# Turning softmax probabilities on one Trainium2 core: a matmul with a scaled diagonal, or a float32 transpose after a GpSimd multiply

## The chip, the cores and the metric

One core of a Trainium2 chip runs the whole kernel. It has a matrix engine (TensorE, PE in the profile; PEld is its weight load), a vector engine (VectorE, DVE), an activation engine (ScalarE, ACT), GpSimd (POOL), and SyncE (SP), which here only issues DMA transfers. Each engine works through its own queue in order and waits on semaphores. The metric is the device time of one execution in microseconds.

## The reference

Four sequences of 512 rows of 512 values (x), and a context of 512 rows of 256 values for each. With LN a layer norm without weights and q(.) a quantization to fp8 with one scale for each 32 values:

```
query = ctx @ Wq.T + bq ;  key = ctx @ Wk.T + bk            (512 x 128 each)
attention = softmax(query @ key.T, axis=-1)                 (512 x 512)
x = x + LN(x) @ attention.T
gate = q(LN(x)) @ q(gate_w).T ;  up = q(LN(x)) @ q(up_w).T  (2048 columns each)
x = x + q(silu(gate) * up) @ q(down_w).T
```

All of it in float32 accuracy. Attention is row n by column m; the product with LN(x) sums over m, so the probabilities have to be turned: m must be on the partitions.

## The kernel before

The kernel is written for each engine as one list of calls whose order was fixed by hand or by a planner; semaphores tie the lists together. b is the sequence (0 to 3), nt a tile of 128 rows of attention, lt a tile of 128 rows of x, u a unit of the feed-forward weights (12 units of 128x2048 values: gate and up alternate in units 0 to 7, down in 8 to 11), r a tile of 128 rows of all 2048 (0 to 15, so r = 4 to 7 is sequence 1), c a quarter of the 2048 hidden columns.

Attention, for each b: PE makes `project` and `energies`; DVE's `row_max` gives the negative maximum of a row; ACT's `exponential` writes exp(energy - max) to `probs[b]` and adds up the row in `esum`; DVE's `row_sum(b)` inverts the four columns of sums into `rsum` (semaphore rsum_ready). Then the probabilities are turned. ACT's `weigh(b, nt)` multiplies the 128x128 identity `idf` by the column `rsum` of that tile, which gives a diagonal matrix. PE's `turn_probs(b, nt)` multiplies each 128x128 block of unscaled exponentials, as the stationary operand, by that diagonal: block.T @ diagonal is the turned block with each column scaled. ACT's `take_probs` copies the bank to `AT`, PE's `attend(b, lt)` multiplies with the columns of x, DVE's `add_attended` adds to x, and its mean and variance are taken for the second norm.

The quantization of the weights goes on beside it, and shares DVE, ACT and POOL with it. For a unit u: SP loads it into one of three places W; DVE: `unit_reduce`, `unit_largest` (column maxima, semaphore smax_ready); POOL: `unit_max(u)` (an all-reduce over the partitions, L575); DVE: `unit_scale`, `unit_power(u)` (L1465, needs the all-reduce), `unit_round` (L1458, L1459, between them ACT's `unit_magnitude`, L926), `unit_dequant` (L1605). ACT's `unit_hi(u)` writes the upper half as float16; POOL's `unit_rest(u)` (L585) issues a DMA that adds it to W and so leaves the remainder; ACT's `unit_lo(u)` writes that. SP turns both halves by transposing DMAs (`turn_unit_hi`, `turn_unit_lo`). POOL's `unit_rest(1)` waits for the transpose of unit 0's lower half, `unit_rest(2)` for that of its own upper half. The rows of x after attention go the same way for each b: DVE's `center`, `rows_scale`, `rows_round`, `rows_dequant`, ACT's `rows_hi` (L1074), POOL's `rows_rest(b)` (L589), ACT's `rows_lo`, SP's `turn_rows_hi` and `turn_rows_lo` into xT. For b > 0 the inverse root of the variance is POOL's `second_norm(b)` (L580, a TENSOR_TENSOR with pow), and `rows_dequant(b)` waits for it.

The feed-forward part on PE is `product(r, c)` (L727: 24 float16 matmuls, gate and up) and `down(r)` (L739, L742). PE's list goes: projections, energies, turns and attends of all b, mixed; `product(3, 0)`, `product(1, 0)`, `product(0, 0)`; `attend(3, ...)`; `product(2, 0)`, `product(3, 1)`, `product(2, 1)`; then `product(6, 0)`, the first that needs the turned rows of sequence 1; and so on to the end. DVE's list around the change:

```python
            unit_power(1)
            row_max(2, 0)
            row_max(2, 1)
            row_sum(1)
            unit_largest(2)
            unit_round(1)
...
            add_attended(2, 0)
            unit_power(3)
            add_attended(2, 1)
```

and POOL's, whole up to where the change ends:

```python
            unit_max(0)
            unit_rest(0)
            unit_max(1)
            unit_max(2)
            unit_rest(1)
            unit_rest(2)
            rows_rest(0)
            unit_max(3)
            unit_max(4)
```

Of the kernel before, what the change touches and what calls it, by code (L numbers as in the profile page):

```python
# [9 lines left out]
ALU = mybir.AluOpType  # L10
ACT = mybir.ActivationFunctionType
AX = mybir.AxisListType

P = 128
# [18 lines left out]
def xattn_ffn(nc, xrows, xcols, ctxT, consts, units, out):  # L33

    B, _, XF = xrows.shape
    H = out.shape[2]
    LT = XF // H
    HT = H // P  # L40
# [52 lines left out]
    with ExitStack() as stack:  # L93
        def sb(name, shape, dt):
            return stack.enter_context(nc.sbuf_tensor(name, shape, dt))
# [4 lines left out]
        def sem(name):  # L100
            return stack.enter_context(nc.semaphore(name))
# [4 lines left out]
        h = sb("h", [P, SLOTS, UNIT], F32)  # L106
# [9 lines left out]
        scale = sb("scale", [P, 3, NB], F32)  # L116
# [21 lines left out]
        probs = [place.rearrange("p (t n) -> p t n", n=512)  # L138
                 for place in (early[:, 0:UNIT], early[:, UNIT:2 * UNIT], *lower)]
# [9 lines left out]
        idf = late[:, 1538:1538 + P]  # L149
        xsum, xnmean, xssq, xlog, xrstd, nmax, esum, rsum = [late[:, 1680 + RT * n:1680 + RT * (n + 1)] for n in range(8)]  # L150
# [2 lines left out]
        xTf = [h[:, 0:LT, 1536:2048], h[:, 0:LT, 1024:1536]]  # L153
        X = [h[:, 4, :], h[:, 6, :], early[:, 3 * UNIT:4 * UNIT],
             gu_hi[:, 2, :, :].rearrange("p g n -> p (g n)").bitcast(F32)]
        diagonal = [[h[:, nt, 512 + n * P:512 + (n + 1) * P] for nt in range(LT)] for n in range(B)]
        early_xw = h[:, 5, :]
        ctx = [place[:, n * 1024:(n + 1) * 1024].rearrange("p (t n) -> p t n", n=512)
               for place in (ctx_all, early_xw) for n in range(2)]
# [58 lines left out]
        rsum_ready = sem("rsum_ready")  # L218
# [3 lines left out]
        xmean_ready = sem("xmean_ready")  # L222
        xstats_ready = [sem(f"xstats{b}_ready") for b in range(B)]
        ymean_ready = sem("ymean_ready")
        diagonal_ready = sem("diagonal_ready")
        last_in = sem("last_in")
        last_ready = sem("last_ready")
        last_summed = sem("last_summed")
# [341 lines left out]
        def _(pool):  # L570
            own = Steps(pool_step)

            def unit_max(u):
                pool.wait_ge(smax_ready, u + 1)
                nc.gpsimd.partition_all_reduce(umax[:, u:u + 1], smax[:, u:u + 1], P,  # L575
                                               bass.bass_isa.ReduceOp.max).then_inc(umax_ready, 1)

            def second_norm(b):
                pool.wait_ge(var_ready[b], 1)
                nc.gpsimd.tensor_tensor(rstd[:, of(b)], var[:, of(b)], mhalf[:, :], ALU.pow).then_inc(rstd_ready[b], 1)  # L580

            def unit_rest(u):

                pool.wait_ge(whi_ready, u + 1)
                nc.gpsimd.dma_start(W[u % 3][:, :], wparts[:, 0, :], accum_op=ALU.add).then_inc(wrest_in, 16)  # L585

            def rows_rest(b):
                pool.wait_ge(nhi_ready, b + 1)
                nc.gpsimd.dma_start(xw_of(b), xparts_of(b)[:, 0, :], accum_op=ALU.add).then_inc(nrest_in, 16)  # L589
# [13 lines left out]
            own.done(nc.gpsimd.memset(eps[:, 1:2], LN_EPS * X_SCALE ** -2))  # L603
            pool.wait_ge(pool_step, own.done(nc.gpsimd.memset(mhalf[:, :], -0.5)))
            unit_max(0)
            unit_rest(0)
            unit_max(1)
            unit_max(2)
            pool.wait_ge(wT_in[1], 16)
            unit_rest(1)  # L610
            pool.wait_ge(wT_in[0], 48)
            unit_rest(2)
            rows_rest(0)
            unit_max(3)
            unit_max(4)
            pool.wait_ge(wT_in[1], 48)
# [60 lines left out]
        def _(pe):  # L677
# [19 lines left out]
            def turn_probs(b, nt):  # L697

                bank = take_bank(f"t{b}.{nt}")
                pe.wait_ge(diagonal_ready, LT * b + nt + 1)  # L700
                for j in range(HT):
                    last = pe.matmul(bank[:, j * P:(j + 1) * P], probs[b][:, nt, j * P:(j + 1) * P],  # L702
                                     diagonal[b][nt], start=(j == 0), stop=(j == HT - 1))
                last.then_inc(probs_turned, 1)

            def attend(b, lt):
# [211 lines left out]
        def _(act):  # L918
# [78 lines left out]
                nc.scalar.activation(probs[b][:, nt, :], bank_of(f"e{b}.{nt}")[:, :], ACT.Exp, bias=nmax[:, row],  # L997
                                     accum_out=esum[:, row]).then_inc(exp_ready, 1)

            def weigh(b, nt):  # L1000

                act.wait_ge(rsum_ready, b + 1)
                nc.scalar.activation(diagonal[b][nt], idf, ACT.Copy, scale=rsum[:, LT * b + nt:LT * b + nt + 1]
                                     ).then_inc(diagonal_ready, 1)

            def take_probs(b, nt):
                if b > 0:
                    act.wait_ge(attended, LT * b)
# [147 lines left out]
            take_projection(2, 0)  # L1156
            take_projection(2, 1)
            row_means(1, 0)
            weigh(0, 0)
            row_means(1, 1)  # L1160
            weigh(0, 1)
            weigh(0, 2)
            unit_hi(0)
            exponential(1, 0)
            weigh(0, 3)
            take_probs(0, 0)
            exponential(1, 1)
            take_probs(0, 1)
# [2 lines left out]
            exponential(1, 3)  # L1171
            take_probs(0, 3)
            unit_magnitude(1)
            weigh(1, 0)
            take_projection(3, 0)
            unit_lo(0)
            weigh(1, 1)
            exponential(2, 0)
            unit_rescale(1)
            exponential(2, 1)  # L1180
# [2 lines left out]
            row_means(2, 0)  # L1183
            take_projection(3, 1)
            unit_hi(1)
            weigh(1, 2)
            unit_magnitude(2)
            exponential(2, 3)
            take_probs(1, 0)
            weigh(1, 3)  # L1190
            unit_rescale(2)
            weigh(2, 0)
            take_probs(1, 1)
            take_probs(1, 2)
            take_probs(1, 3)
            weigh(2, 1)
            row_means(3, 0)
            unit_lo(1)
            attended_variances(0, 0)
# [2 lines left out]
            row_variances(2, 0)  # L1202
            rows_magnitude(0)
            unit_hi(2)
            weigh(2, 2)
            attended_variances(0, 1)
            exponential(3, 0)
            weigh(2, 3)
            take_probs(2, 0)
            exponential(3, 1)  # L1210
            take_probs(2, 1)
# [6 lines left out]
            row_variances(3, 0)  # L1218
            exponential(3, 3)
            row_variances(2, 1)  # L1220
            weigh(3, 0)
            weigh(3, 1)
            weigh(3, 2)
            weigh(3, 3)
            unit_magnitude(3)
            rows_lo(0)
            row_variances(3, 1)
# [741 lines left out]
```

## Time and profile before

| | |
|---|---|
| median of 3 runs | 608.89 us (608.5 to 609.56) |
| span of the profiled execution | 608.0 us, 0.9 under the median of the runs |
| PE busy | 600.6 us, 99% |
| DVE busy | 484.0 us, 80% |
| ACT busy | 309.2 us, 51% |
| POOL busy | 44.8 us, 7% |

The profile is of one execution; its span runs from the first to the last instruction. What lies around the span (the start and the end of the program) isn't in it, and the runs' times hold it. A busy share is an average over the whole span: the four engines don't have the same share in the first 140 us as later, and a queue that is seldom busy can still be what another engine waits for.

### The profile page before, as it was taken

The page shows a single profiled execution, that of the slowest core. Times are in us where ns is not written, and L with a number is a line of the kernel's source. Part 1 is how long each engine was busy: PE and PEld are TensorE (multiplying, and loading weights), DVE is VectorE, ACT ScalarE, POOL GpSimd, SP SyncE. Part 2 cuts the span into 40 slices and gives each one's busy share as a digit, 9 for nine tenths or more (in the row PEclk, how much of TensorE's full clock was granted, in tenths as well). Part 3 has the DMA queues.
Part 4 walks back from the last instruction along what each step waited for, and adds up shares of the span by engine and source line. Part 5 has one row for each costly group of instructions (what it writes and reads, how often), then busy time and mean ns, then how long its engine had stood idle before and what let it go on. Part 6 is the DMA issues. An engine that isn't in the chain of part 4 may idle for free.

```text
span 608.0 us, 7215 instructions
## 1 busy us (share of the span) xinstructions
PE 600.6 (99%) x2683; PEld 282.3 (46%) x2683; DVE 484.0 (80%) x455; ACT 309.2 (51%) x463; POOL 44.8 (7%) x60
## 2 busy tenths in 40 slices
PE   8999999999999999999999999999999999999998
PEld 3456554444444444444444444444444444444446
DVE  4999998899999999988999985131148899989740
ACT  3999989553555555853475532431121515254520
POOL 0000002100000001010110201000000000001100
PEclk9999999999999999999999999999999999999999
DMA  8989869989988978867445655750010334557691
GB/s 314 396 206 275 234 177 256 280 193 249 208 207 209 219 159 210 174 140 171 124 112 97 148 112 113 165 86 0 1 19 0 53 69 83 90 105 101 110 171 35
DMA packets 148162, 92.28 MB, mean 152 GB/s; under 512 B 134304, under 2 KB 134688, under 8 KB 143264
## 3 DMA queue, kind: packets, MB, share of 16 engines
q1 hardware_dynamic: 142656, 63.78, 45.2%
q0 software_dynamic: 5472, 28.05, 19.9%
q8 instruction: 21, 0.34, 0.2%
q14 instruction: 13, 0.11, 0.1%
HBM read 25.76 MB, written 8.39 MB: 56 GB/s over the span
## 4 chain that ended last, share of the span: by engine, by line
PE 85%; DMA 5%; issue 3%; ACT 3%; DVE 1%; SPq 1%; POOL 0%; DVEq 0%; ACTq 0%
PE bank L727 49%; PE bank L739 17%; PE bank L742 9%; PE bank L711 5%; DMA h<-in_ctxT 2%; PE bank L702 1%; PE bank L695 1%; DMA xT<-hT 1%; PE bank L687 1%; PE bank L757 1%; DMA W<-hT 1%; DMA h<-hT 1%; ACT hT L944 1%; PE bank L762 1%; ACT h L987 0%
## 5 line engine op out<-in xcount | busy, mean ns | idle before, releaser
L727 PE MATMUL bank<-gu_hi,xT 128*128 128x512 f16 x1024 | 243.6, 380 | 1.7 <-DMA xT<-hT 1.7
L727 PEld LDWEIGHTS bank<-gu_hi,xT 128*128 128x128 f16 x1024 | 99.9, 98 | 123.4 <-DMA xT<-hT 3.2
L727 PE MATMUL bank<-gu_lo,xT 128*128 128x512 f16 x512 | 131.5, 379 | 0.0
L739 PE MATMUL bank<-dn,hT 128*128 128x512 f16 x480 | 106.1, 379 | 0.0
L1633 DVE SCALAR_TENSOR_TENSOR h<-bank,unscale,silu 128x512 f32<-128x512 f32 x64 | 47.4, 747 | 56.1 <-PE bank L727 36.1
L1088 ACT ACTIVATE silu<-bank,unscale 128x512 f32<-128x512 f32 x64 | 42.8, 679 | 83.4 <-PE bank L727 40.3
L727 PEld LDWEIGHTS bank<-gu_lo,xT 128*128 128x128 f16 x512 | 50.1, 98 | 60.4
L739 PEld LDWEIGHTS bank<-dn,hT 128*128 128x128 f16 x480 | 47.0, 98 | 56.6
L1114 ACT ACTIVATE W<-h 128x2048 f16<-128x2048 f32 x16 | 30.5, 1909 | 68.3 <-DVE W L1665 25.4
L711 PE MATMUL bank<-dn,h 128*128 128x512 f32 x128 | 55.9, 593 | 0.0
L742 PE MATMUL bank<-dn,hT 128*128 128x512 f16 x240 | 54.3, 379 | 0.0
L1458 DVE SCALAR_TENSOR_TENSOR h<-mag,h 128x2048 f32<-128x2048 bf16 x18 | 41.2, 2288 | 9.4 <-ACT mag L926 9.4
L926 ACT ACTIVATE mag<-h 128x2048 bf16<-128x2048 f32 x18 | 34.2, 1903 | 19.5 <-DVE h L1647 14.1
L1459 DVE SCALAR_TENSOR_TENSOR h<-mag,h 128x2048 f32<-128x2048 bf16 x18 | 41.2, 2292 | 0.6
L926 ACT ACTIVATE mag<-W 128x2048 bf16<-128x2048 f32 x14 | 26.7, 1908 | 23.0 <-DVE W L1590 11.9
L711 PEld LDWEIGHTS bank<-dn,h 128*128 128x128 f32 x128 | 24.3, 190 | 29.8 <-issue 29.4
L1665 DVE SCALAR_TENSOR_TENSOR W<-h,W 128x2048 f16<-128x2048 f32 x9 | 20.6, 2289 | 20.9 <-DMA hT<-W 17.4
L1647 DVE TENSOR_TENSOR h<-h,rscale 128x2048 f32<-128x2048 f32 x16 | 36.7, 2292 | 0.5
L1642 DVE TENSOR_REDUCE hscale<-h 128x64 f32<-128x2048 f32 x16 | 36.5, 2281 | 0.3
L1659 DVE TENSOR_TENSOR h<-h,hscale 128x2048 f32<-128x2048 f32 x16 | 36.6, 2288 | 0.2
L742 PEld LDWEIGHTS bank<-dn,hT 128*128 128x128 f16 x240 | 23.5, 98 | 28.3
L1458 DVE SCALAR_TENSOR_TENSOR W<-mag,W 128x2048 f32<-128x2048 bf16 x14 | 32.0, 2286 | 1.0 <-ACT mag L926 1.0
(119 smaller groups left out, 560.1 us busy)
## 6 DMA issues: line engine op xcount, KB each, us to landing
W<-hT POOLq DMA_DIRECT2D x12, 1024.0 KB, 5.9
W<-in_units SPq DMA_DIRECT2D x11, 1024.0 KB, 5.7
h<-W POOLq DMA_DIRECT2D x7, 1024.0 KB, 6.1
h<-in_xcols SPq DMA_DIRECT2D x4, 1024.0 KB, 12.6
out_y<-y POOLq DMA_DIRECT2D x12, 256.0 KB, 6.2
h<-in_xrows SPq DMA_DIRECT2D x2, 1024.0 KB, 11.8
out_y<-h SPq DMA_DIRECT2D x2, 1024.0 KB, 5.5
h<-hT POOLq DMA_DIRECT2D x2, 1024.0 KB, 5.9
```

What stands on the lines that cost most here:

```text
L711: last = pe.matmul(bank[:, :], xTf[b % 2][:, j, lt * P:(lt + 1) * P], AT[:, j, :], start=(j == 0), stop=(j == HT - 1))
L727: last = pe.matmul(bank[:, :], xT[:, b % 2, part, k, :], w[:, c, g, j * 512:(j + 1) * 512], start=(j == 0 and not low), stop=(j == HT - 1 ...
L739: pe.matmul(bank[:, :], hT[:, r % 2, 0, k, :], dn[:, w, k, :], start=(k == 0 and w == 0), stop=False)
L742: last = pe.matmul(bank[:, :], hT[:, r % 2, 1, k, :], dn[:, 0, k, :], start=False, stop=(k == IT - 1))
L926: nc.scalar.activation(mag[:, :], v, ACT.Abs, scale=MAGIC).then_inc(mag_ready, 1)
L1088: nc.scalar.activation(silu[:, n % 2, :], bank_of(f"g{r}.{c}")[:, :], ACT.Silu, scale=unscale[:, 2 * c:2 * c + 1]).then_inc(silu_ready, 1)
L1458: then(dve.scalar_tensor_tensor(v, mag[:, :], floor, v, ALU.max, ALU.add))
L1459: dve.scalar_tensor_tensor(v, mag[:, :], floor, v, ALU.max, ALU.subtract).then_inc(mag_used, 1)
L1633: dve.scalar_tensor_tensor(hrow(r)[:, c * 512:(c + 1) * 512], bank_of(f"u{r}.{c}")[:, :], unscale[:, 2 * c + 1:2 * c + 2], silu[:, n % 2, ...
L1642: then(dve.tensor_reduce(s, blocks(row), AX.X, ALU.max, apply_absolute_value=True))
L1647: dve.tensor_tensor(blocks(row), blocks(row), each_block(rscale[:, :]), ALU.mult).then_inc(hv_ready, 1)
L1659: dve.tensor_tensor(blocks(row), blocks(row), each_block(hscale[:, r % 2, :]), ALU.mult).then_inc(hd_ready, 1)
```

## The change

PE's turn becomes a transpose of the block against the plain identity. The scaling by the inverse row sums is done before, by GpSimd, in place in `probs[b]`, four instructions of 128x512 for each b, at four places of POOL's list. ACT's 16 scalings of the identity are gone, and so is the diagonal's space. DVE's list is the same.

```diff
--- before.py
+++ after.py
-        diagonal = [[h[:, nt, 512 + n * P:512 + (n + 1) * P] for nt in range(LT)] for n in range(B)]
...
+            def weigh(b, nt):
+                pool.wait_ge(rsum_ready, b + 1)
+                row = slice(LT * b + nt, LT * b + nt + 1)
+                nc.gpsimd.tensor_scalar(probs[b][:, nt, :], probs[b][:, nt, :], rsum[:, row], None, ALU.mult
+                                        ).then_inc(normal_ready, 1)
...
             unit_max(0)
+            weigh(0, 0)
+            weigh(0, 1)
+            weigh(0, 2)
+            weigh(0, 3)
             unit_rest(0)
             unit_max(1)
             unit_max(2)
+            weigh(1, 0)
+            weigh(1, 1)
+            weigh(1, 2)
+            weigh(1, 3)
             pool.wait_ge(wT_in[1], 16)
             unit_rest(1)
+            weigh(2, 0)
+            weigh(2, 1)
+            weigh(2, 2)
+            weigh(2, 3)
             pool.wait_ge(wT_in[0], 48)
             unit_rest(2)
             rows_rest(0)
+            weigh(3, 0)
+            weigh(3, 1)
+            weigh(3, 2)
+            weigh(3, 3)
             unit_max(3)
             unit_max(4)
...
             def turn_probs(b, nt):
 
                 bank = take_bank(f"t{b}.{nt}")
-                pe.wait_ge(diagonal_ready, LT * b + nt + 1)
+                pe.wait_ge(normal_ready, LT * b + nt + 1)
                 for j in range(HT):
-                    last = pe.matmul(bank[:, j * P:(j + 1) * P], probs[b][:, nt, j * P:(j + 1) * P],
-                                     diagonal[b][nt], start=(j == 0), stop=(j == HT - 1))
+                    last = pe.transpose(bank[:, j * P:(j + 1) * P], probs[b][:, nt, j * P:(j + 1) * P], idf)
                 last.then_inc(probs_turned, 1)
...
-            def weigh(b, nt):
-
-                act.wait_ge(rsum_ready, b + 1)
-                nc.scalar.activation(diagonal[b][nt], idf, ACT.Copy, scale=rsum[:, LT * b + nt:LT * b + nt + 1]
-                                     ).then_inc(diagonal_ready, 1)
```

The other lines of the diff take the 16 `weigh` calls out of ACT's list and rename the semaphore.

## Rows read from the trace of the kernel before

**Rows 1.** The profile page, busy time and granted clock in 40 slices.
```profile
PE 600.6 (99%) x2683; PEld 282.3 (46%) x2683; DVE 484.0 (80%) x455; ACT 309.2 (51%) x463; POOL 44.8 (7%) x60
...
PEclk9999999999999999999999999999999999999999
```
**Rows 2.** Busy time by stretch: stretch, PE, PEld, DVE, ACT, POOL, clock, DMA share.
```profile
20.00:92.00 72.00, 71.67 (x262) 39.66 (x260) 69.01 (x87) 67.24 (x151) 4.84 (x7) 1.00 0.87 247
...
140.00:606.00 466.00, 465.07 (x2203) 215.11 (x2200) 359.32 (x309) 199.69 (x251) 31.49 (x38) 1.00 0.58 120
```
**Rows 3.** The chain of waits in order of time: start, us, what.
```profile
49.99 4.46 PE bank L702 x40
...
138.57 134.85 PE bank L727 x624
```
**Rows 4.** PE in order of time, with the idle time before.
```profile
92.60 1.04 PE L727 MATMUL bank<-gu_hi,xT 128*128 128x512 f16 x4 [0.93 <-DMA xT<-hT]
...
138.57 1.04 PE L727 MATMUL bank<-gu_hi,xT 128*128 128x512 f16 x4 [0.32 <-DMA xT<-hT]
```
**Rows 5.** DVE in order of time, then one group of its instructions by form.
```profile
23.45 2.26 DVE L1605 TENSOR_TENSOR W<-W,scale 128x2048 f32<-128x2048 f32 x1
...
33.36 0.15 DVE L1465 TENSOR_SCALAR pow<-umax 128x1 int32<-128x1 int32 x1
...
35.09 0.22 DVE L1583 TENSOR_REDUCE smax<-scale 128x1 f32<-128x64 f32 x1
36.29 2.29 DVE L1458 SCALAR_TENSOR_TENSOR W<-mag,W 128x2048 f32<-128x2048 bf16 x1 [0.98 <-ACT mag L926]
...
86.17 0.15 DVE L1465 TENSOR_SCALAR pow<-umax 128x1 int32<-128x1 int32 x1
...
92.70 2.28 DVE L1605 TENSOR_TENSOR W<-W,scale 128x2048 f32<-128x2048 f32 x1
...
106.88 2.29 DVE L1458 SCALAR_TENSOR_TENSOR h<-mag,h 128x2048 f32<-128x2048 bf16 x1 [2.31 <-ACT mag L926]
...
112.52 0.23 DVE L1549 TENSOR_TENSOR xscale<-xscale,rstd 128x64 f32<-128x64 f32 x1 [1.02 <-POOL rstd L580]
...
L1522 DVE TENSOR_SCALAR h<-h,nmean 128x512 f32<-128x512 f32 x4 | 1.7, 482 | 0.0
```
**Rows 6.** POOL in order of time, with the idle time before.
```profile
29.52 1.18 POOL L585 DMA_DIRECT2D W<-hT  x1 [17.73 <-ACT hT L944]
...
47.61 0.88 POOL L585 DMA_DIRECT2D W<-hT  x1 [11.85 <-ACT hT L944]
71.57 0.85 POOL L585 DMA_DIRECT2D W<-hT  x1 [23.09 <-DMA gu_hi<-hT]
82.44 0.88 POOL L589 DMA_DIRECT2D h<-hT  x1 [10.01 <-issue]
...
92.87 2.32 POOL L575 PARTITION_ALL_REDUCE umax<-smax  x1 [9.22 <-DVE smax L1583]
...
110.53 1.89 POOL L580 TENSOR_TENSOR rstd<-var,mhalf 128x4 f32<-128x4 f32 x1 [6.75 <-issue]
...
131.49 0.38 POOL L575 PARTITION_ALL_REDUCE umax<-smax  x1 [5.84 <-issue]
...
268.20 1.21 POOL L580 TENSOR_TENSOR rstd<-var,mhalf 128x4 f32<-128x4 f32 x1 [7.85 <-issue]
```
**Rows 7.** ACT in order of time.
```profile
75.44 1.89 ACT L1074 ACTIVATE hT<-h 128x2048 f16<-128x2048 f32 x1
...
83.56 1.26 ACT L1003 ACTIVATE h<-gu_lo 128x128 f32<-128x128 f32 x4
```
**Rows 8.** Lines 575 and 580: count, ns min/median/max, first and last start in us.
```profile
L575 POOL PARTITION_ALL_REDUCE umax<-smax x12: 339/350/2317, 11.4 to 211.4; - x12
L575 POOLq MODIFY_POOL_CONFIG  x4: 11/182/349, 1.1 to 125.6; - x4
...
L580 POOLq MODIFY_POOL_CONFIG  x4: 349/356/363, 103.5 to 260.1; - x4
```

More of the change, by code:

```diff
@@ L224, in xattn_ffn @@
         ymean_ready = sem("ymean_ready")
-        diagonal_ready = sem("diagonal_ready")
+        normal_ready = sem("normal_ready")
         last_in = sem("last_in")
@@ L1158, in _ @@
             row_means(1, 0)
-            weigh(0, 0)
             row_means(1, 1)
-            weigh(0, 1)
-            weigh(0, 2)
             unit_hi(0)
             exponential(1, 0)
-            weigh(0, 3)
             take_probs(0, 0)
@@ L1173, in _ @@
             unit_magnitude(1)
-            weigh(1, 0)
             take_projection(3, 0)
             unit_lo(0)
-            weigh(1, 1)
             exponential(2, 0)
@@ L1185, in _ @@
             unit_hi(1)
-            weigh(1, 2)
             unit_magnitude(2)
@@ L1189, in _ @@
             take_probs(1, 0)
-            weigh(1, 3)
             unit_rescale(2)
-            weigh(2, 0)
             take_probs(1, 1)
@@ L1195, in _ @@
             take_probs(1, 3)
-            weigh(2, 1)
             row_means(3, 0)
@@ L1204, in _ @@
             unit_hi(2)
-            weigh(2, 2)
             attended_variances(0, 1)
             exponential(3, 0)
-            weigh(2, 3)
             take_probs(2, 0)
@@ L1220, in _ @@
             row_variances(2, 1)
[L1221 to L1224, printed above, removed]
             unit_magnitude(3)
```

## The prediction

> **What bounds the kernel now.** I read the page first. TensorE (PE) is busy for 600.6 of 608.0 us and its granted clock is full in every slice [rows 1]. From 140 to 606 us it works 465.07 of 466 us [rows 2], so nothing after 140 us can be shortened by this change, which touches only the attention part at the start. The chain of waits says where that dense part begins: at 138.57 us, at PE's first matmul on the x rows of sequence 1 (`product(6, 0)`), and it waited there for the DMA xT<-hT [rows 3, 4]. So the end is the moment at which sequence 1's second normalized rows are turned, plus about 468 us. PE also waited for DMA at 92.60 us, at `product(3, 0)` [rows 4]. Both gaps are short: PE and the chain that feeds it arrive almost together.
>
> The feeding chain is next. VectorE (DVE) is busy 69.01 of 72 us between 20 and 92 us, ScalarE (ACT) 67.24 [rows 2]. DVE's own order leaves few holes: 0.98 us at 36.29, 2.31 at 106.88, 1.02 at 112.52 [rows 5]. Its order is fixed, and two of its short instructions take what GpSimd (POOL) makes: `unit_power(1)` at 33.36 and `unit_power(3)` at 86.17 read the result of a partition all-reduce [rows 5]. POOL itself is almost idle, 7%, but it is a queue, and the rows to look at are the idle times inside it [rows 6].
>
> **TensorE.** A turn is eight matmul records now; 40 of them took 4.46 us, 0.11 each, so 0.89 us a turn and 14.3 us for 16 [rows 3]. The float32 transpose doesn't occur in the trace. Upper bound: the same 0.89. Lower bound: one pass. A 128x512 f16 matmul takes 134.85/624 = 0.216 us, a quarter of that for 128 columns is 0.054, four make 0.22 us a turn. I take the lower end, 10.7 us less for PE. None of it reaches the end by itself: PE at 92.60 and 138.57 waits for transfers that it doesn't make [rows 4].
>
> **ScalarE.** Sixteen 128x128 activations go; four took 1.26 us together [rows 7], about 0.3 each, 4.8 in all. What DVE can get of it is the 0.98 us wait for ACT at 36.29 and the 2.31 at 106.88 [rows 5].
>
> **GpSimd: the multiply.** 16 TENSOR_SCALAR of 128x512 f32 in place; call one w. No such row on POOL. Lower bound: DVE's TENSOR_SCALAR of that shape, 0.48 us [rows 5]. Upper: the only elementwise arithmetic on POOL, TENSOR_TENSOR with pow, took 1.21 and 1.89 us for four columns [rows 6]. POOL's arithmetic is slow in the one row that exists, so I take w = 1.9; four are 7.6 us. The Trainium skill (GPSIMD Engine Reference, 4.1 Engine selection) says that one-input elementwise work is roughly line-rate there; as an estimate from that page 512 elements at 1.2 GHz would be 0.43 us, the sum below would then end near its low case. No row decides.
>
> **GpSimd: the reload.** The trace has MODIFY_POOL_CONFIG at L580 (pow) and L575 (all-reduce), four records of each [rows 8]; the long idle times stand where one kind follows the other. After it the engine sits: 6.75 us before 110.53; 5.84 before the all-reduce at 131.49, although its input came earlier; 7.85 before 268.20 [rows 6]. Mean 6.8 us. I take TENSOR_SCALAR to need the same code as TENSOR_TENSOR. The Trainium skill (GPSIMD Engine Reference, 2.1 Instruction dispatch) gives about 6 us for the first call of a freshly loaded kernel; rows here show 5.8 to 7.9. In the new POOL order there are four more changes: all-reduce 0, weigh(0), (DMA), all-reduces 1 and 2, weigh(1), weigh(2), (DMAs), weigh(3), all-reduce 3. The first (before weigh(0)) lies in the 17.73 us for which POOL now waits before 29.52 [rows 6]. The other three lie on paths that DVE or PE waits for.
>
> **GpSimd against VectorE.** The all-reduce at 92.87 took 2.32 us where the others take 0.35, beside a DVE TENSOR_TENSOR with two SBUF inputs that began at 92.70 [rows 5, 6]. So a POOL instruction can be held for the rest of such a DVE instruction, up to 2.29 us, and presumably the reverse. The Trainium skill (SBUF, State Buffer: Who interferes with whom) has this as an exclusive lock; the trace agrees with 2.32 against 0.35.
>
> **The sum**, in the order of POOL's queue:
> - A. weigh(0) may start when DVE's L1605 (23.45, about 2.26) lets go, 25.7; four end at 33.3. unit_rest(0)'s DMA issue 0.9: 34.2 (before 29.5). Reload 6.8: 41.0. All-reduce 1, 0.4: 41.4. unit_power(1) stood at 33.36: DVE is 8.0 late, then 7.0, as the 0.98 wait goes.
> - B. DVE's maximum of unit 2 (35.09 + 0.22) is at 43.3, all-reduce 2 done 43.7, reload to 50.5, weigh(1) 7.6 plus one DVE instruction of 2.3 in the way: 60.4. unit_rest(1) is queued behind it: before 47.61, so 12.8 late. PE's turns of sequence 1 (49.99) wait as well.
> - C. unit_rest(2) at 71.57 waits for the transpose that follows unit_rest(1) [rows 6]; the same distance gives 84.4. weigh(2) (61.3 to 69, or later) fits before it.
> - D. rows_rest(0): its input ended at 75.44 + 1.89 = 77.33 [rows 7] and is 7.0 late, but it stood 10.87 behind unit_rest(2). Between 85.2 (only queued behind it) and 95.2 (same distance); I take the middle, 90.2.
> - E. Issue 0.9, weigh(3) 7.6, reload 6.8, all-reduce 0.4: unit_power(3) can run at 105.9, against 86.17. DVE is 19.7 late. PE's product(3,0), fed by rows_rest(0), is some 8 late and no longer matters.
> - F. Everything of DVE up to the rows of sequence 1 shifts. It gets back 2.31 (ACT's magnitude) and 1.02 (pow; its own reload is not new): 16.4 late at 112.8. From there ACT, unit_rest(4) and the transpose at 130 to 138 follow in the same distances, and PE's dense part begins 16.4 us later.
>
> The profiled span is 608.0, the median of the runs 608.89; adding to the median, 608.9 + 16.4 = 625.3 us.
>
> **Range.** Low: w = 0.48, reload 5.8, nothing held. Then A is +3.3 (DVE +2.3 after its gain), B puts unit_rest(1) at 49.9, D lies between 80 and 84.8, E gives 89.0 to 93.8, and after F it is -0.5 to +4.3: 608.4 to 613.2. High: w = 2.3, reload 7.85, D at its upper end: A +10.7, B 65.8 (+18.2), D 100.6, E 119.0, F +29.5: 638.4. The corner at the bottom needs all favourable values together, so I give 612 to 638.
>
> **Rivals.**
> 1. No reload, long multiply. If TENSOR_SCALAR runs under either configuration, only w counts. weigh(0) delays the all-reduce to 34.6 (+1.2); weigh(3) runs 83.3 to 90.9, all-reduce 3 ends 91.3, unit_power(3) +5.1, less 3.3: +1.8, 610.7. For it: MEMSETs run without a reload of their own. Against it: the one elementwise arithmetic instruction has one. Chance 0.05.
> 2. Faster: no reload and a short multiply. The same path with w = 0.48: all-reduce 3 is there at 85.6, before DVE wants it, and DVE keeps the 0.98 and 2.31 that ACT's lighter queue returns: -3, 606. It decides below w = (86.17+3.3-83.3-0.4)/4 = 1.4 us. Chance 0.04.
> 3. PE's 10.7 us reach the end: 598. It asks that the transfers at 92.60 and 138.57 come earlier; DVE at 96% forbids it. Chance 0.01.
> 4. The clock. PE now waits in long pieces (some 8 us at product(3,0), again before 138.57). No row shows the lower level: it is 1.00 throughout. If PE restarts at 1.2 GHz, the first product (24 matmuls, 5.2 us) takes 10.4: forecast + 5, 631; decisive only if it stays low. The Trainium skill (TensorE: Matmul & The Clock Gate, Part 4) says that transposes don't count as activity for the clock, which would make that likelier; no row of this trace has one. Chance 0.05.
> 5. All favourable values at once with reloads, within 0.2% (1.2 us, about what three runs can tell): 0.03.
>
> **How the numbers follow.** Forecast with reloads, slower: 0.82. Slower in all 0.82+0.05+0.05 = 0.92, faster 0.04+0.01 = 0.05, same 0.03. The range 612 to 638 leaves out rivals 1 to 3 and 5 and the tails, under 0.2.
>
> **What the profile after should show.** MODIFY_POOL_CONFIG also at the multiply's line, four more changes. POOL's idle time before all-reduce 1 and 3 of 6 to 8 us. DVE idle before L1465 twice: some 8 us near 33, some 10 to 18 near 90, released by POOL. w of 1.9, turns of 0.22 us on PE. PE idle before product(3,0) and before product(6,0), which starts near 155; nothing changed behind it. I am wrong if L1465 doesn't wait, or if the gap before product(6,0) is filled by something of DVE's that I took to be late with it.

## The result and the profile after

The changed kernel takes 624.08 us (median of 4 runs, 623.84 to 624.93) against 608.72 of the kernel before (4 runs). The ratio is 1.024, with an interval of 1.0223 to 1.0257: slower by some 15 us. The forecast was 625.3, its range 612 to 638. The profiled execution took 624.04 with a span of 622.2, which is 14.2 us more than the span of the profile before. In every execution of the later comparisons the time is 1.7 to 2.1 us above the span. By that the execution profiled before, with its span of 608.0, was one of the longer ones of its kernel, near 610 us (an estimate), and this is why the spans differ by 1 us less than the medians.

The page of the kernel after, to be held against [rows 1]:

```profile
PE 601.2 (97%) x2619; PEld 276.8 (44%) x2619; DVE 486.9 (78%) x455; ACT 305.9 (49%) x447; POOL 76.6 (12%) x76
...
PEclk9996999999999999999999999999999999999999
```

PE lost 64 records and is busy no shorter: a slice now has a lower granted clock. POOL is 31.8 us busier, 29.5 of it the multiplies. Busy time by stretch, the columns as in [rows 2]:

```profile
20.00:92.00 72.00, 62.98 (x170) 29.72 (x169) 61.86 (x75) 57.48 (x127) 30.18 (x19) 0.91 0.77 226
...
154.00:620.00 466.00, 465.28 (x2204) 215.38 (x2201) 359.55 (x309) 199.85 (x251) 32.09 (x38) 1.00 0.58 120
```

Between 20 and 92 us DVE does 7.15 us less in the same time: it did not get faster, it waits. ACT does 9.76 us less, of which 5.9 are the 16 scalings that are gone (L1003 in the trace before); the rest is waiting too. The dense part, looked at 14 us later than before, is the old one to 0.2 us. So all is decided before it. POOL in order of time, to be held against [rows 6]:

```profile
23.08 8.16 POOL L584 TENSOR_SCALAR dn<-dn,gu_lo 128x512 f32<-128x512 f32 x4 [11.86 <-DVE gu_lo L1490]
...
38.21 0.38 POOL L574 PARTITION_ALL_REDUCE umax<-smax  x1 [5.86 <-issue]
...
51.30 6.64 POOL L584 TENSOR_SCALAR dn<-dn,gu_lo 128x512 f32<-128x512 f32 x4 [8.31 <-issue]
57.89 1.05 POOL L590 DMA_DIRECT2D W<-hT  x1
58.70 8.18 POOL L584 TENSOR_SCALAR gu_lo<-gu_lo 128x512 f32<-128x512 f32 x4
79.85 0.89 POOL L590 DMA_DIRECT2D W<-hT  x1 [12.96 <-DMA gu_hi<-hT]
90.25 0.88 POOL L594 DMA_DIRECT2D h<-hT  x1 [9.52 <-issue]
90.83 6.51 POOL L584 TENSOR_SCALAR gu_lo<-gu_lo 128x512 f32<-128x512 f32 x4
103.37 0.38 POOL L574 PARTITION_ALL_REDUCE umax<-smax  x1 [6.03 <-issue]
```

In front of each all-reduce or multiply that follows the other kind the engine stands idle for "issue", 5.86, 8.31 and 6.03 us. Four multiplies take 6.5 to 8.2 us. `unit_rest(1)` went from 47.61 to 57.89, `unit_rest(2)` from 71.57 to 79.85, `rows_rest(0)` from 82.44 to 90.25. DVE, against [rows 5]:

```profile
38.62 0.15 DVE L1463 TENSOR_SCALAR pow<-umax 128x1 int32<-128x1 int32 x1 [5.75 <-POOL umax L574]
...
103.78 0.15 DVE L1463 TENSOR_SCALAR pow<-umax 128x1 int32<-128x1 int32 x1 [7.94 <-POOL umax L574]
...
126.75 0.23 DVE L1547 TENSOR_TENSOR xscale<-xscale,rstd 128x64 f32<-128x64 f32 x1
```

`unit_power(1)` is 5.3 us late, `unit_power(3)` 17.6; both wait for POOL. The last line stood at 112.52 and had waited 1.02 us; it no longer waits and is 14.2 us late, as much as the span has grown. PE, against [rows 4]:

```profile
61.25 1.08 PE L723 MATMUL bank<-gu_lo 128*128 128x128 f32 x4 [2.08 <-POOL gu_lo L584]
...
79.44 0.60 PE L723 MATMUL bank<-gu_lo 128*128 128x128 f32 x4
...
96.51 1.91 PE L723 MATMUL bank<-gu_lo 128*128 128x128 f32 x16
100.59 1.04 PE L747 MATMUL bank<-gu_hi,xT 128*128 128x512 f16 x4 [2.16 <-DMA xT<-hT]
...
121.75 15.67 PE L731 MATMUL bank<-dn,h 128*128 128x512 f32 x32 [2.89 <-ACT dn L1024]
```

A turn is now four records of 0.11 us, 0.45 us in all, where it was eight. PE waits for POOL's multiplies, and `product(3, 0)` stands at 100.59 instead of 92.60. Last, the chain of waits (start, us, what):

```profile
51.30 6.64 POOL dn L584 x4
57.94 1.00 POOL W L590
...
84.24 1.90 ACT hT L1088
86.14 4.11 issue
90.25 0.88 POOL h L594
91.14 6.21 POOL gu_lo L584 x4
97.34 0.24 POOLq L574 x2
97.59 5.78 issue
103.37 0.39 POOL umax L574
103.76 0.02 issue
103.78 0.17 DVE pow L1463
```

From `rows_rest(0)` (90.25) on it reads plainly: `weigh(3)`, a reload, all-reduce 3, `unit_power(3)`. Before it the chain names ACT's `rows_hi(0)` (L1088), and then has 4.11 us of "issue", for which it names nothing. Another transfer ends in that gap. `unit_rest(2)` was issued at 79.85 and took 10.1 us to land, so it landed at 90.0, and `rows_rest(0)` starts right behind. These lines of ACT, SP and the DMA show where `unit_rest(2)` comes from:

```profile
63.86 1.91 ACT L970 ACTIVATE hT<-W 128x2048 f16<-128x2048 f32 x1 [2.78 <-DMA W<-hT]
...
73.31 1.90 ACT L964 ACTIVATE hT<-W 128x2048 f16<-128x2048 f32 x1
```
```profile
75.23 1.98 SPq L400 DMA_TRANSPOSE gu_hi<-hT  x1
```
```profile
W<-hT POOLq DMA_DIRECT2D x1, 1024.0 KB, 10.1
```

ACT's `unit_lo(1)` (L970) waits until `unit_rest(1)` has landed, 5.9 us after its issue at 57.89. From there to the end of `unit_hi(2)` (L964, 75.2) ACT works without a wait. Then SP turns unit 2's upper half (75.23), and `unit_rest(2)` follows at 79.85. In the kernel before, `unit_lo(1)` began at 55.67 and `unit_hi(2)` at 65.11, at the same distance of 9.4 us. So the way is: reload, `weigh(1)`, `unit_rest(1)`, ACT, the transpose, `unit_rest(2)`, its landing, `rows_rest(0)`, `weigh(3)`, reload, all-reduce 3. That is the forecast's path. Experiment 9 shows what stands close beside it.

### The profile page after: what moved, and what is told of

Same layout as the page of the kernel before. It is cut to its first block, busy times and chain, and to the rows that moved or that the text cites. A ratio compares the mean times of both kernels' runs of the same rounds, so it can differ in the third digit from the quotient of the medians.

```text
span 622.2 us, 7095 instructions
## 1 busy us (share of the span) xinstructions
PE 601.2 (97%) x2619; PEld 276.8 (44%) x2619; DVE 486.9 (78%) x455; ACT 305.9 (49%) x447; POOL 76.6 (12%) x76
## 3 DMA queue, kind: packets, MB, share of 16 engines
q0 software_dynamic: 5472, 28.05, 19.7%
## 4 chain that ended last, share of the span: by engine, by line
PE 83%; DVE 5%; POOL 5%; issue 4%; ACT 2%; DMA 1%; SPq 0%; POOLq 0%; DVEq 0%; ACTq 0%
PE bank L747 51%; PE bank L759 17%; PE bank L762 8%; PE bank L731 5%; POOL dn L584 2%; POOL gu_lo L584 1%; PE bank L777 1%; DVE W L1456 1%; DMA W<-in_units 1%; DVE W L1457 1%; DVE gu_lo L1485 1%; PE bank L782 1%; POOL umax L574 0%; PE bank L716 0%; DVE h L1535 0%
## 5 line engine op out<-in xcount | busy, mean ns | idle before, releaser
L747 PEld LDWEIGHTS bank<-gu_lo,xT 128*128 128x128 f16 x512 | 50.1, 98 | 60.4
L731 PE MATMUL bank<-dn,h 128*128 128x512 f32 x128 | 57.7, 607 | 2.9 <-ACT dn L1024 2.9
L970 ACT ACTIVATE hT<-W 128x2048 f16<-128x2048 f32 x12 | 22.9, 1906 | 23.1 <-DMA W<-hT 23.1
```

The costliest lines, as they stand in the source:

```text
L731: last = pe.matmul(bank[:, :], xTf[b % 2][:, j, lt * P:(lt + 1) * P], AT[:, j, :], start=(j == 0), stop=(j == HT - 1))
L747: last = pe.matmul(bank[:, :], xT[:, b % 2, part, k, :], w[:, c, g, j * 512:(j + 1) * 512], start=(j == 0 and not low), stop=(j == HT - 1 ...
```

## The experiments

The theory: GpSimd's queue is full. Four more changes of instruction kind cost a reload each, four groups of multiplies some 7 us each, in series with DMA issues and all-reduces that others wait for. Rivals were that the reload alone does it, that the multiply alone does it, that PE's transposes do, and that the clock does.

**1. Only the reload** (on the kernel before; `touch(b)` stands where the changed kernel has `weigh(b, ...)`):
```diff
+            def touch(b):
+                pool.wait_ge(rsum_ready, b + 1)
+                nc.gpsimd.tensor_scalar(probe[:, b:b + 1], mhalf[:, 0:1], rsum[:, LT * b:LT * b + 1], None, ALU.mult)
```


> The kernel before, with one GpSimd multiply of a single column (128x1) at each of the four places where the changed kernel has its four multiplies; ScalarE's diagonals and TensorE's matmuls stay. The column goes to a tile that nothing reads. Reload theory: the reloads alone hold VectorE's unit_power(1) some 3 us (29.5 + 0.9 + 5.8 + 0.4 = 36.6 against 33.4) and unit_power(3) some 7 us (82.4 to 85 for rows_rest(0), 0.9, 5.8, 0.4), less the 3.3 us of waits that VectorE gets back: 612 to 614 us, 3 to 5 over the kernel before. Multiply theory (GpSimd's 16 times 1.6 us, not the reload, made the loss): within 1 us of before. TensorE theory (transposes and the clock made it): within 1 us of before.

Measured: 611.12 against 609.66, ratio 1.0032 (1.0011 to 1.0053). The reloads are there and DVE waits for them, but the end moves by only 1.5 to 2 us, less than the theory of the reload had:
```profile
37.44 0.15 DVE L1474 TENSOR_SCALAR pow<-umax 128x1 int32<-128x1 int32 x1 [3.59 <-POOL umax L576]
...
90.71 0.15 DVE L1474 TENSOR_SCALAR pow<-umax 128x1 int32<-128x1 int32 x1 [2.86 <-POOL umax L576]
```

**2. Only the multiplies** (on the kernel after; the all-reduce becomes a copy, so no cross-partition maximum is formed and POOL never changes its kind around the multiplies):
```diff
-                nc.gpsimd.partition_all_reduce(umax[:, u:u + 1], smax[:, u:u + 1], P,
-                                               bass.bass_isa.ReduceOp.max).then_inc(umax_ready, 1)
+                nc.gpsimd.tensor_scalar(umax[:, u:u + 1], smax[:, u:u + 1], 1.0, None, ALU.mult
+                                        ).then_inc(umax_ready, 1)
```


> The changed kernel with the cross-partition all-reduce left out: unit_max copies each partition's own maximum by a GpSimd multiply of 128x1 by 1.0, so that GpSimd never changes its code. The 16 multiplies of 128x512 stay. Reload theory: unit_power(1) no longer waits (weigh(0) ends near 31), unit_power(3) can run near 91 (82.5 + 0.9 + 6.5 to 8 + 0.4) and VectorE gets its small waits back: 607 to 611 us, at least 13 of the 15.4 us of loss gone. Multiply theory: most of the loss stays, 618 to 623. TensorE or clock theory: 620 or more.

Measured: 608.66 against 609.66, 0.9984 (0.9967 to 1.0001). Same multiplies, same transposes, no loss. POOL's rows show the gap gone and a group of multiplies held even longer than in the kernel after:
```profile
38.18 11.56 POOL L584 TENSOR_SCALAR dn<-dn,gu_lo 128x512 f32<-128x512 f32 x4
49.69 0.87 POOL L590 DMA_DIRECT2D W<-hT  x1
51.46 10.08 POOL L584 TENSOR_SCALAR gu_lo<-gu_lo 128x512 f32<-128x512 f32 x4 [0.90 <-DVE gu_lo L1490]
```
The multiply alone is refuted as the cause. The pow of `second_norm(1)` follows a multiply here and waited only 0.77 us, for its input: between these two kinds there is no reload.

**3. The control for 2** (the diff of 2, on the kernel before; it too forms no cross-partition maximum):

> The kernel before with the same substitution as in e2 (each partition's own maximum in place of the all-reduce), as the control for e2. All theories: 606 to 608.7 us; it loses the reload in front of second_norm(1), for which VectorE waited 1.02 us at 112.52, and the one in front of unit_max(5). The difference e2 minus e3 is then the price of the multiplies and transposes without reload: reload theory 0 to +4, multiply theory +10 or more.

Measured: 610.03, ratio 0.9998 (0.9983 to 1.0014). Sparing the kernel before its own reloads gives nothing, so experiment 2's gain isn't that of a kernel without all-reduces.

**4. All the reloads, almost no multiply** (on the kernel after; all but the first column of each tile stays unscaled):
```diff
-                nc.gpsimd.tensor_scalar(probs[b][:, nt, :], probs[b][:, nt, :], rsum[:, row], None, ALU.mult
+                nc.gpsimd.tensor_scalar(probs[b][:, nt, 0:1], probs[b][:, nt, 0:1], rsum[:, row], None, ALU.mult
```


> The changed kernel with each of the 16 multiplies cut to one column (128x1), so that the order, the waits, the transposes and the reloads stay and 511 of 512 columns remain unscaled. Reload theory: unit_power(1) still waits about 4 us and unit_power(3) about 5 to 7; what goes is four multiplies in each of three places on the way, about 6 us in each, not all in a row: 612 to 616 us. Multiply theory: 606 to 609. TensorE theory: 620 or more.

Measured: 609.26, ratio 0.9995 (0.9982 to 1.0009), below what was expected. The reload alone is refuted too. Each part fits by itself into the time for which POOL has nothing to do; together they don't. DVE does wait 2.82 and 3.06 us for the two all-reduces, but against them stands what the lighter PE and ACT are worth, 3.5 to 3.9 us (experiment 6).

**5. The turn by a matmul with the identity instead of the transpose** (on the kernel after):
```diff
-                    last = pe.transpose(bank[:, j * P:(j + 1) * P], probs[b][:, nt, j * P:(j + 1) * P], idf)
+                    last = pe.matmul(bank[:, j * P:(j + 1) * P], probs[b][:, nt, j * P:(j + 1) * P],
+                                     idf, start=(j == 0), stop=(j == HT - 1))
```


> The changed kernel with TensorE's float32 transposes made by ordinary float32 matmuls against the identity (two records for a block instead of one, 0.89 us a turn instead of 0.45, 7.1 us more TensorE work in all). Theory of the full queue (GpSimd's reloads and multiplies stand in one row and only together outgrow the idle time of its queue): the turns lie beside waits, 623 to 625 us as the changed kernel. TensorE theory (the transposes, or the clock that they leave low, have a part in the loss): below 622.

Measured: 624.69 against 609.55, 1.0271 (1.0235 to 1.0308), an interval that overlaps that of the kernel after. How PE turns is not the cause.

**6. What the lighter PE and ACT are worth** (on the kernel after; all 16 `weigh` calls are left out, so nothing is scaled):
```diff
             unit_max(0)
-            weigh(0, 0)
-            weigh(0, 1)
...
-                pe.wait_ge(normal_ready, LT * b + nt + 1)
+                pe.wait_ge(rsum_ready, b + 1)
```

> The changed kernel without its multiplies and without their waits: TensorE turns the unscaled exponentials as soon as the row sums are inverted, GpSimd's list is that of before, ScalarE's diagonals stay away. Left out is the division by the row sums. All that TensorE (7.1 us) and ScalarE (4.8 us) save is in, and nothing of what was added. Theory of the full queue: VectorE's order and the transfers bound it, 605 to 608 us, 1 to 3 under the kernel before. If TensorE's saving reaches the end: 600 to 602.

Measured: 605.66 against 609.55, 0.9942 (0.9921 to 0.9964). So the most the change could have gained, with its new work free of charge, is 3.5 us by the ratio, 3.9 by the medians. Its page shows the full granted clock in all 40 slices.

**7. ACT multiplies in place, PE transposes** (a form with all of the computation, on the kernel before):
```diff
-                nc.scalar.activation(diagonal[b][nt], idf, ACT.Copy, scale=rsum[:, LT * b + nt:LT * b + nt + 1]
+                nc.scalar.activation(probs[b][:, nt, :], probs[b][:, nt, :], ACT.Copy,
+                                     scale=rsum[:, LT * b + nt:LT * b + nt + 1]
```


> The kernel before with ScalarE multiplying the exponentials by the inverse row sums in place (16 activations of 128x512 at about 0.6 us instead of 16 of 128x128 at 0.3) at the same 16 places of its list, and TensorE turning them by transposes. GpSimd is as before. ScalarE was busy for 67 of 72 us between 20 and 92 us and gets 4.5 us more; TensorE gets 7.1 less. If ScalarE's extra time reaches VectorE's waits: 609 to 613 us. If it finds holes: 607 to 609. TensorE's saving at the end would be 602 or less.

Measured: 610.09, 1.002 (1.0005 to 1.0035). ACT is busy 71.14 of 72 us between 20 and 92, DVE 67.83 and PE 67.20: ACT is now the fullest engine there, and nothing of PE's saving is seen at the end. That ACT uses it up is argued from these shares, not shown.

**8. All-reduce 3 ahead of `rows_rest(0)`** (on the kernel after):
```diff
             unit_rest(2)
+            unit_max(3)
             rows_rest(0)
...
             weigh(3, 3)
-            unit_max(3)
             unit_max(4)
```

> The changed kernel with one call moved: the all-reduce of unit 3 stands before rows_rest(0) and weigh(3) on GpSimd, not behind them. Its reload then runs while GpSimd waits for rows_rest(0)'s input, and VectorE's unit_power(3) finds it done; but weigh(3) and unit_max(4) each get a reload in front. Theory of the full queue: the wait of 7.94 us at unit_power(3) is gone and one of 4 to 6 us comes at unit_power(4), 618 to 622 us. If the multiply's time alone counted, no change: 624.

Measured: 627.04, 1.0289 (1.0264 to 1.0314): a miss, it is slower than the kernel after. The wait only moved, from `unit_power(3)` to `unit_power(4)`, and there is one change of kind more, so two reloads now lie around `weigh(3)`:
```profile
99.52 8.71 POOL L584 TENSOR_SCALAR gu_lo<-gu_lo 128x512 f32<-128x512 f32 x4 [7.20 <-issue]
115.99 0.38 POOL L574 PARTITION_ALL_REDUCE umax<-smax  x1 [7.76 <-issue]
```
```profile
116.40 0.15 DVE L1463 TENSOR_SCALAR pow<-umax 128x1 int32<-128x1 int32 x1 [11.14 <-POOL umax L574]
```

**9. `unit_rest(1)` ahead of `weigh(1)`**, with the reload begun by a 128x1 multiply (on the kernel after):
```diff
             unit_max(2)
+            nc.gpsimd.tensor_scalar(probe[:, :], mhalf[:, 0:1], 1.0, None, ALU.mult)
+            pool.wait_ge(wT_in[1], 16)
+            unit_rest(1)
             weigh(1, 0)
...
-            pool.wait_ge(wT_in[1], 16)
-            unit_rest(1)
             weigh(2, 0)
```


> The changed kernel with unit_rest(1) in front of weigh(1) in GpSimd's list, and a one-column multiply (128x1) of a constant behind unit_max(2), so that the reload still runs at that place. Tests step B of the prediction (unit_rest(1) queued behind four multiplies makes rows_rest(0) and what follows late). If B holds: unit_rest(1) at about 51.5 instead of 57.9, rows_rest(0) some 4 to 6 us earlier, 618 to 620 us. If rows_rest(0) is held by something else: 623 to 625.

Measured: 623.64 against 609.34, 1.0237 (1.0214 to 1.026): a miss. `unit_rest(1)` came 6.2 us earlier, yet `rows_rest(0)` only 2.3:
```profile
51.70 1.04 POOL L591 DMA_DIRECT2D W<-hT  x1
...
78.31 0.90 POOL L591 DMA_DIRECT2D W<-hT  x1 [10.17 <-DMA gu_hi<-hT]
87.98 0.88 POOL L595 DMA_DIRECT2D h<-hT  x1 [8.77 <-ACT hT L1090]
```
```profile
81.09 0.60 ACT L1026 ACTIVATE dn<-bank 128x512 f32<-128x512 f32 x1 [4.74 <-PE bank L733]
...
85.69 1.89 ACT L1090 ACTIVATE hT<-h 128x2048 f16<-128x2048 f32 x1
```
Two things come out of it. First, `unit_rest(2)` moved only 1.5 us, to 78.31, because ACT reaches `unit_lo(1)` only at 62.38: the transfer it needs has landed by 57.7, but ACT is still at its copies of sequence 1's turns, and these wait for POOL's multiplies. The second road to `unit_rest(2)`, by PE's and ACT's operands, is thus just 1.5 us behind the first in the kernel after. Second, `rows_rest(0)` is held here by ACT's `rows_hi(0)` (L1090); ACT stands for 4.74 us for PE's attend, and `unit_rest(2)` has landed 2.8 us before `rows_hi(0)` ends. In the kernels without this edit it is the other way round (all times in us, landing is issue plus the time to landing):

| kernel | `unit_rest(2)` at | landed | `rows_hi(0)` ended | `rows_rest(0)` at |
|---|---|---|---|---|
| before | 71.57 | 82.2 | 77.3 | 82.44 |
| 4, one column | 73.31 | 80.2 | 78.4 | 80.50 |
| 12, full for sequence 3 | 72.86 | 81.0 | 77.5 | 81.30 |
| after | 79.85 | 90.0 | 86.1 | 90.25 |
| 9, unit_rest(1) first | 78.31 | 84.8 | 87.6 | 87.98 |

In 13 of the 14 traces of this case `rows_rest(0)` starts 0.3 us after the landing of `unit_rest(2)`; in the 14th, experiment 9, `rows_hi(0)` ended later and it starts 0.4 us after that. `weigh(3)` then waits 3.38 us for the row sums of sequence 3, and with the reload behind it all-reduce 3 stands at 104.80, 1.4 us later than in the kernel after. So one road was shortened, and the other took its place.

**10. The clock** (on the kernel after; eleven products with the identity, 22 records, ahead of `attend(3)`, so that PE doesn't stand still):
```diff
             product(0, 0)
+            keep("a3.0", 11)
             attend(3, 0)
```


> The changed kernel with 11 float32 matmuls of the identity with itself (128x128, 0.22 us each, results overwritten) between product(0, 0) and attend(3, 0), where TensorE stood idle for 2.89 us and then took 15.5 us for attend(3), with a granted clock of 0.90 in that stretch, against 13.7 in the kernel before. Clock theory: attend(3) is back at 13.7 to 13.9 us, 1.5 to 1.8 us less: 622.3 to 622.6. If VectorE's order or the transfers hold product(6, 0) anyway: 624.

Measured: 623.8, 1.0239 (1.022 to 1.0257). The attends of sequence 3 now run in 13.97 us instead of 15.67. The median is 0.3 us under that of the kernel after, which the intervals don't tell from nothing. In this trace `product(6, 0)` waits for its transfer:
```profile
122.94 13.97 PE L731 MATMUL bank<-dn,h 128*128 128x512 f32 x32 [0.43 <-ACT dn L1025]
...
152.63 1.04 PE L747 MATMUL bank<-gu_hi,xT 128*128 128x512 f16 x4 [0.18 <-DMA xT<-hT]
```

In the trace of the kernel after it doesn't: the transfer was issued at 144.84 and took 6.4 us, so it landed at 151.3, and PE came to it only at 152.8, straight from the attends. Up to 1.5 us of that execution can so be the clock's; here, where all-reduce 3 stood 1.2 us later, the transfer landed at 152.6 and used them up.

**11. A smaller POOL share** (all of the computation, on the kernel before: POOL instead of ACT makes the diagonals, 128x128 each, at the four places):
```diff
+            def weigh(b):
+                pool.wait_ge(rsum_ready, b + 1)
+                for nt in range(LT):
+                    nc.gpsimd.tensor_scalar(diagonal[b][nt], idf, rsum[:, LT * b + nt:LT * b + nt + 1], None, ALU.mult
+                                            ).then_inc(diagonal_ready, 1)
```


> The kernel before with its 16 diagonals made by GpSimd (128x128 multiplies of the identity) instead of ScalarE, at the four places where the changed kernel has its multiplies; TensorE's matmuls with the diagonal stay. Reloads as in the changed kernel, a quarter of the multiply's columns, each about 0.6 us by the rows of 1 column (0.25) and 512 columns (1.56). Theory of the full queue, in series and without a threshold: one column gave 609.3, 512 gave 624.1, so 128 columns give 609.3 + 14.8 * (0.6 - 0.25) / (1.56 - 0.25) = 613; with a threshold in the idle time of the queue: 609 to 611.

Measured: 614.93 (9 runs, 611.43 to 616.12), 1.0073 (1.005 to 1.0097). A quarter of the multiply's size already costs 4 to 6 us, where a single column with the same PE work, and ACT's scalings kept, cost 1.5 to 2 (experiment 1): the loss grows with the work from the start, as work in series does. The runs spread over 4.7 us, so its size is known only roughly.

**12. The full multiply for sequence 3 alone** (on the kernel after; for sequences 0 to 2 only the first column of each tile is scaled):
```diff
+                n = 512 if b == 3 else 1
+                nc.gpsimd.tensor_scalar(probs[b][:, nt, 0:n], probs[b][:, nt, 0:n], rsum[:, row], None, ALU.mult
```


> The changed kernel with the multiplies of sequences 0 to 2 cut to one column and those of sequence 3 whole (sequences 0 to 2 stay unscaled but for one column). With all cut (one column everywhere) rows_rest(0) stood at 80.50, all-reduce 3 at 90.00, median 609.26; changed kernel 90.25, 103.37, 624.1. If the loss is two pieces in series (upstream: the multiplies of 1 and 2 delay TensorE's turn of sequence 2, ScalarE's copies of it, rows_hi(0) queued behind them, and so rows_rest(0) by 9.75 us; then weigh(3) itself, 5.5 us longer, in front of the second reload): rows_rest(0) at 80.5 to 81, weigh(3) from 83 to 89.3, all-reduce 3 at 95.6, 614 to 615 us. If weigh(3) were all of it: 622 or more. If the upstream piece alone: 609 to 610.

Measured: 614.76 against 610.19, 1.0073 (1.0048 to 1.0099), as expected. POOL's rows show `weigh(3)` and the reload in series in front of all-reduce 3:
```profile
81.30 0.89 POOL L595 DMA_DIRECT2D h<-hT  x1 [7.54 <-issue]
82.19 6.22 POOL L585 TENSOR_SCALAR gu_lo<-gu_lo 128x512 f32<-128x512 f32 x4
94.53 0.38 POOL L574 PARTITION_ALL_REDUCE umax<-smax  x1 [6.12 <-issue]
```
The loss is so in two pieces: `weigh(3)` 5.0 to 5.5 us, the multiplies of sequences 0 to 2 9.3 to 10.8 (by the medians 609.26, 614.76 and 624.08, or by each one's difference to the kernel before beside it). The second piece enters at `unit_rest(1)`, 49.34 here and 57.89 in the kernel after, 8.6 us, and reaches `rows_rest(0)`, 81.30 and 90.25, as 9.0.

**Together.** One number orders them roughly: when `unit_power(3)` starts (86.17 before), against what the median gained or lost. It doesn't order neighbours (11 and 12, the kernel after and 9, change places), and it fails for experiment 8, whose wait is at `unit_power(4)`.

| kernel | unit_power(3) at | late by | median, less that of before |
|---|---|---|---|
| 6, no multiply | 84.08 | -2.1 | -3.9 |
| 2, no reload | 88.97 | +2.8 | -1.0 |
| 4, one column | 90.42 | +4.3 | -0.4 |
| 1, reload only | 90.71 | +4.5 | +1.5 |
| 11, 128x128 | 93.83 | +7.7 | +5.6 |
| 12, full for sequence 3 | 94.94 | +8.8 | +4.6 |
| after | 103.78 | +17.6 | +15.4 |
| 9, unit_rest(1) first | 105.20 | +19.0 | +14.3 |

Some 2 to 5 us of the lateness are given back behind it; [rows 5] show 2.31 and 1.02 us as waits, which a late DVE no longer has.

Counted from experiment 6, where nothing new is asked of POOL (-3.9), the reloads alone add 3.5 us (4), the multiplies alone 2.9 (2), both together 19.3. `unit_rest(1)` shows why. It had 11.85 us of idle time in front of it, from all-reduce 2 on [rows 6]. The multiplies alone (experiment 2) put it at 49.69, the reload alone (4) at 49.99, some 2 us late each. In the kernel after a reload of 8.31 us and multiplies of 6.64 make 15, 3.1 more than the idle time; and all-reduce 2 itself ended at 42.98 instead of 35.75, 7.2 late, by `weigh(0)` and the reload behind it. So `unit_rest(1)` stands at 57.89, 10.3 late.

## Why the prediction was right, and where it was off

**Right.** TENSOR_SCALAR does need the reload after an all-reduce: records of MODIFY_POOL_CONFIG stand at the multiply's line (four) and four more at the all-reduce's:
```profile
L574 POOLq MODIFY_POOL_CONFIG  x8: 11/323/349, 1.1 to 139.8; - x8
...
L584 POOLq MODIFY_POOL_CONFIG  x4: 82/83/83, 11.2 to 43.0; - x4
```
Its size, 6.8 us, was 5.9 to 8.3. Both DVE waits came where the forecast had them, and both were shorter than it had them, 5.75 (some 8 forecast) and 7.94 (10 to 18). `rows_rest(0)` came at 90.25 (90.2). The 2.31 and 1.02 us did come back. The dense part starts 14.2 us later (16.4) and is unchanged. Rivals 1 and 2 fall by the reloads; rival 5 by the time; rival 3 by experiment 6, which gives 3.5 us where it had 10.7. The medians differ by 15.4 us, 16.4 were forecast.

**A, B: sizes.** w is 1.56 us unheld, where 1.9 was taken; with the holding by DVE a group takes 6.5 to 8.2 (7.6 taken), so it hardly matters. `weigh(0)` began at 23.08 and not at 25.7: DVE's instruction didn't hold it back from starting, it lengthened the group. That is most of why all-reduce 1 came at 38.2 (41.0) and `unit_rest(1)` at 57.9 (60.4).

**C and D: the path was right, its two sizes were not, and luck set them off.** The forecast led from `unit_rest(1)` through the transposes and `unit_rest(2)` to `rows_rest(0)`, and this is the way the traces show. C had `unit_rest(2)` at 84.4, 12.8 late; it stood at 79.85, 8.3 late. Of the 4.6 us too much, 2.5 are B's, and the rest is mostly that ACT came to `unit_lo(1)` 1.8 us after the landing in the kernel before (55.67 against 53.8) and at once in the kernel after: that slack took up part of the delay. D put `rows_rest(0)` between "only queued behind it" and "same distance" (10.87 us) and took the middle, 5.8 us. The distance was 10.40: the upper bound was right, since what `rows_rest(0)` follows is the landing of `unit_rest(2)`. Some 4.6 us too much in C and 4.6 too little in D gave 90.2 against 90.25. That agreement is luck, and with the whole distance in D the forecast would have been 5 us higher.

The forecast had also seen that "PE's turns of sequence 1 wait as well" and drew nothing from it. In the kernel after this second road decides nothing, but experiment 9 shows it 1.5 us behind the first: whoever had repaired only the first would have gained 1.5 us at `unit_rest(2)` and not 6.2.

**E:** `unit_power(3)` is 17.6 us late, 19.7 forecast. `weigh(3)`, a reload and the all-reduce took 13.5 us from `rows_rest(0)`, 15.7 forecast (w again, and the reload 6.0).

**The turn.** 0.45 us, between the bounds 0.22 and 0.89; the saving is 7.1 us and not 10.7. It changed nothing, as the forecast said: experiment 5.

**The clock.** Rival 4 expected a price of 5 us from the lower level of 1.2 GHz. The lower clock came, 0.69 of full between 44 and 66 us, after PE had stood 3.84 us for the multiply, and 0.90 between 121 and 138, after 2.89 us for ACT. It lengthened the attends of sequence 3 by 1.8 us and cost at most 1.5 us at the end, and nothing that the medians show (experiment 10). The Trainium skill (TensorE: Matmul & The Clock Gate, Part 4) says that transposes don't count as activity for the clock. Two runs bear on it. Experiment 5 has much the same waits for POOL and ordinary matmuls in the place of the transposes, and between 44 and 66 us its clock is 0.92 and not 0.69, which agrees with the page, though PE is also busy 16.1 us there instead of 14.3. Experiment 6 has all the transposes and none of the waits, and the full clock in every slice. So the longest stretch at the lower level came where transposes and waits came together. The wait that the forecast had in front of `product(6, 0)` wasn't there: PE came 1.5 us after the transfer had landed, from the attends of sequence 3 that had waited for ACT.

**Not foreseen at all:** that reload and multiply cost almost nothing apart (-1.0 to +1.5 us) and 15.4 together. The prediction's sum has both in one series and so came out right, but its expectations for one part alone, written with the experiments, were too high for 1 and 4.

**Small.** From 138.57 to the end are 469.4 us and not about 468; nothing hangs on it. The 16 scalings of ACT took 5.9 us together and not 4.8.

**Open.** Why `rows_rest(0)` waits for the landing of `unit_rest(2)`'s transfer isn't shown: the kernel asks for it by no semaphore, and at 256.13 in the kernel after a DMA of POOL starts 2.2 us before the one issued ahead of it has landed. Nor is it shown why this transfer took 10.1 us (10.6 before, 6.5 in experiment 9) where the median of its line is 5.9; a load of 1 MB issued 0.2 us ahead of it (0.7 before) is a rival that wasn't tried. Nor was a kernel in which both `unit_rest(1)` and the first turns are early. No version with the whole computation beats the kernel before: 7 is at 1.002, 11 at 1.0073.

## What to carry to other kernels

An engine that is 7% busy can still be full at one place: add what is put into its queue to what already stands between two of its results that others wait for, and compare with the idle time there, not with the idle time of the whole. On GpSimd count the changes of instruction kind first, here six to nine microseconds each, then the work. Where one delay reaches a point by two roads (a DMA queue, another engine's operands), work out both: the later one is the answer, and the other says how much a repair of it can give. And where the chain of waits has some microseconds of "issue" right before a DMA, look when the DMA issued ahead of it landed.

## What the runs showed of the hardware

- A GpSimd TENSOR_SCALAR multiply in float32 took 1.56 us for 128x512, 0.59 for 128x128 (2.34 and 2.37 for four) and 0.26 for 128x1 (experiment 9): about 2.5 ns for each further column. DVE's TENSOR_SCALAR of 128x512 takes 0.48 [rows 5]. The Trainium skill (GPSIMD Engine Reference, 4.1) calls one-input work roughly line-rate; the trace does not agree.
- The reload took 5.7 to 8.6 us in nearly all places of all runs, 5.7 to 7.8 before an all-reduce, 6.8 to 7.9 before the pow and 7.2 to 8.6 before a multiply; 9.57 stand once before a multiply (experiment 1) and 9.28 once before an all-reduce (experiment 8). It can lie in a wait: the group of multiplies at 23.08 started as soon as its input was there. The Trainium skill (GPSIMD Engine Reference, 2.1) gives about 6 us; the shortest rows agree, the longest are 3.6 us over it.
- Of two DMAs of GpSimd one right behind the other in its list, `unit_rest(2)` and `rows_rest(0)`, the second started 0.3 us after the first had landed, in 13 of 14 traces (table in experiment 9).
- POOL and DVE hold each other: a group of four multiplies took 6.19 us unheld (experiment 2) and up to 11.56 beside DVE's long two-input instructions; a 128x1 multiply took 2.25 (experiment 1). DVE is held as well: its 128x4 TENSOR_SCALAR at 94.17 took 1.68 us beside the multiply:
```profile
94.17 1.68 DVE L1507 TENSOR_SCALAR nmean<-ysum 128x4 f32<-128x4 f32 x1
```
- A float32 transpose leaves one record of 0.11 us for each 128x128 block, a float32 matmul two.
